# A decoder layer on one core: low parts of Wo on GpSimd in halves, TensorE's blocks of Wo five and three, pair 0's low part ahead of a scaling

## What is computed

```python
def _L0_attn_ref(x, w_qkv, w_o):
    ...
    qkv = x @ w_qkv
    ...
    xq = _apply_rope(xq)
    xk = _apply_rope(xk)
    keys = jnp.repeat(xk, N_REP, axis=1)
    values = jnp.repeat(xv, N_REP, axis=1)
    scores = jnp.einsum('bhsd,bhtd->bhst', xq, keys) * scale
    scores = jnp.where(causal, scores, -jnp.inf)
    probs = jax.nn.softmax(scores, axis=-1)
    out = jnp.einsum('bhst,bhtd->bhsd', probs, values)
    return out @ w_o

x = _layernorm(x + _L0_attn_ref(x, L0_attn_w_qkv, L0_attn_w_o), axis=-1)
```

## Time and profile before

| what | value |
|---|---|
| median of three runs | 1260.17 us (1259.99 to 1262.92) |
| profiled execution, its time | 1260.07 us |
| its span, first to last instruction | 1258.0 us |
| mean granted TensorE clock | 0.997 |
| TensorE busy | 1229.6 us (98%), 8134 matmuls |
| VectorE busy | 860.1 us (68%) |
| ScalarE busy | 580.6 us (46%) |
| GpSimd busy | 617.7 us (49%) |

### The profile page before, as it was taken

How to read it: one execution, slowest core, us unless ns; L and a number is a source line. 1 busy time by engine, 2 the same in 40 slices (tenths; PEclk the granted TensorE clock), 3 DMA queues, 4 the chain that set the end, 5 groups by cost and what they waited for, 6 DMA issues and landing times.

```text
span 1258.0 us, 25027 instructions
## 1 busy us (share of the span) xinstructions
PE 1229.6 (98%) x8134; PEld 1038.5 (83%) x8134; DVE 860.1 (68%) x2509; ACT 580.6 (46%) x1659; POOL 617.7 (49%) x522
## 2 busy tenths in 40 slices
PE   8999999999999999999999999999999999899997
PEld 6888889998788888888877887888888888678886
DVE  7999989565778888888776974253453635755654
ACT  5131213556777777777860222252342525532322
POOL 3512112458676776776750000454456554975552
PEclk9999999999999999999999999999999999999999
DMA  8154435364864344344443113317252444723221
GB/s 287 70 201 146 148 116 203 119 197 130 223 190 136 119 140 140 117 133 141 125 132 106 53 34 127 125 67 267 68 180 89 165 170 158 260 85 117 85 83 67
DMA packets 130833, 173.67 MB, mean 138 GB/s; under 512 B 36672, under 2 KB 91968, under 8 KB 130112
## 3 DMA queue, kind: packets, MB, share of 16 engines
q1 hardware_dynamic: 130752, 172.62, 42.2%
HBM read 115.94 MB, written 56.62 MB: 137 GB/s over the span
## 4 chain that ended last, share of the span: by engine, by line
PE 69%; POOL 14%; issue 10%; DMA 2%; DVE 2%; ACT 1%; SPq 1%; POOLq 0%; DVEq 0%; ACTq 0%
PE bank L773 14%; PE bank L775 13%; PE bank L774 13%; POOL prob L2165 10%; PE bank L859 5%; PE bank L1204 4%; PE bank L1206 4%; PE bank L1205 4%; PE bank L824 3%; PE bank L964 3%; POOL att_lo L2171 2%; PE bank L782 1%; PE bank L901 1%; PE bank L886 1%; PE bank L855 1%
## 5 line engine op out<-in xcount | busy, mean ns | idle before, releaser
L2165 POOL TENSOR_TENSOR prob<-prob,rinv 128x512 f32<-128x512 f32 x192 | 206.8, 1078 | 147.4 <-DVE rinv L1755 147.4
L1326 ACT ACTIVATE prob<-bank,nmax 128x256 f32<-128x256 f32 (+1 forms) x512 | 211.6, 429 | 76.0 <-DVE nmax L1747 70.0
L1747 DVE CUSTOM_DVE_ANT_0 bank<-bank,mask 128x256 f32<-128x256 f32 (+1 forms) x512 | 170.1, 385 | 38.0 <-PE bank L886 24.7
L901 PE MATMUL bank<-ident,prob 128*128 128x128 f32 x768 | 115.4, 273 | 1.3 <-ACT probT L1256 0.7
L901 PEld LDWEIGHTS bank<-ident,prob 128*128 128x128 f32 x768 | 94.5, 141 | 25.2 <-POOL prob L2165 2.4
L1326 ACT ACTIVATION_READ_ACCUMULATOR prob<-bank,nmax 128x1 f32 x512 | 109.7, 214 | 0.0
L964 PE MATMUL bank<-wo_hi,att_hi 128*128 128x512 f32 x256 | 104.3, 407 | 2.6 <-issue 2.6
L1902 DVE SCALAR_TENSOR_TENSOR k_lo<-bank,bA,k_hi 128x512 fp32r<-128x512 f32 x32 | 24.0, 751 | 120.9 <-ACT k_hi L1459 119.2
L886 PE MATMUL bank<-k,q 96*128 96x256 f32 (+1 forms) x512 | 104.2, 305 | 1.3 <-DMA vv<-v_scr 1.3
L964 PE MATMUL bank<-wo_hi,att_lo 128*128 128x512 f32 x256 | 101.3, 396 | 0.0
L964 PE MATMUL bank<-wo_lo,att_hi 128*128 128x512 f32 x256 | 101.2, 395 | 0.0
(11 more groups left out here) (221 smaller groups left out, 3247.0 us busy)
## 6 DMA issues: line engine op xcount, KB each, us to landing
q<-qk_scr SPq DMA_DIRECT2D x192, 128.0 KB, 2.4
x_st<-x_scr SPq DMA_DIRECT2D x32, 512.0 KB, 4.1
qk_scr<-rot SPq DMA_DIRECT2D x60, 256.0 KB, 2.6
xc_in<-x_cols SPq DMA_DIRECT2D x32, 256.0 KB, 4.7
y<-x SPq DMA_DIRECT2D x16, 512.0 KB, 3.6
x_scr<-y SPq DMA_DIRECT2D x16, 512.0 KB, 2.7
cx_in<-ctx_in SPq DMA_DIRECT2D x16, 512.0 KB, 4.9
x_scr<-x_st SPq DMA_DIRECT2D x16, 512.0 KB, 3.3
```

The costliest lines, as they stand in the source:

```text
L901: mm = nc.tensor.transpose(tb[:, at * P:(at + 1) * P], prob[:, k % 4, c:c + P], ident[:, :])
L1326: mm = nc.scalar.activation(prob[:, k % 4, i * keys:(i + 1) * keys], SBANK[pos][:, i * keys:(i + 1) * keys], ACT.Exp, bias=nmax[:, k % 4, ...
L1747: mm = nc.vector.tensor_tensor_reduce(part, part, mask[:, 2 * P - keys:2 * P], 1.0, BIGGEST, ALU.add, ALU.min, nmax[:, k % 4, i:i + 1])
L2165: nc.gpsimd.tensor_tensor(pr, pr, rinv[:, k % 4, 0:n].unsqueeze(2).to_broadcast([P, n, keys]), ALU.mult)\
```

## The change

Four things. The low parts of all eight blocks of Wo are taken by GpSimd, in halves of 512 columns with one semaphore (`wo_low`, `WO_LOW_STEPS`); block 5 goes from step 22 of batch 0 to step 3 of batch 1, blocks 6 and 7 come from VectorE to steps 5, 7 and 8 of batch 1. ScalarE makes the high parts of blocks 6 and 7 two steps earlier. TensorE takes five blocks for the first portion of `g` 0 and 1 and three for the second, and waits for both halves of a block. In every batch GpSimd takes the low part of outputs of pair 0 ahead of the scaling of step 23 instead of behind it.

```diff
-        LOW_STEP = {23: (0, 0), 0: (1, 1), 2: (1, 2), 6: (1, 3)}
-        WO_STEPS = {(0, 12): 2, (0, 14): 3, (0, 18): 0, (0, 19): 1, (0, 20): 4, (0, 21): 5, (1, 5): 6, (1, 7): 7}
-        WO_EARLY = sum(age == 0 for age, _ in WO_STEPS)
+        LOW_STEP = {0: (1, 1), 2: (1, 2), 6: (1, 3)}
+        WO_STEPS = {(0, 12): 2, (0, 14): 3, (0, 18): 0, (0, 19): 1, (0, 20): 4, (0, 21): 5, (1, 3): 6, (1, 5): 7}
+        WO_LOW_STEPS = {(0, 13): ((2, 0), (2, 1)), (0, 15): ((3, 0), (3, 1)), (0, 19): ((0, 0), (0, 1)), (0, 20): ((1, 0), (1, 1)),
+                        (0, 21): ((4, 0), (4, 1)), (1, 3): ((5, 0), (5, 1)), (1, 5): ((6, 0), (6, 1)), (1, 7): ((7, 0),),
+                        (1, 8): ((7, 1),)}
...
-            WO = [(g, kt, ps) for kts in (range(KT - 2), range(KT - 2, KT)) for g in (0, 1) for kt in kts for ps in range(3)]
+            WO = [(g, kt, ps) for kts in (range(KT - 3), range(KT - 3, KT)) for g in (0, 1) for kt in kts for ps in range(3)]
...
                     if g == 0 and ps == 0:
-                        if WO_TURN[kt] < WO_EARLY:
-                            pe.wait_ge(wo_lo_ready, WO_TURN[kt] + 1)
-                        else:
-                            pe.wait_ge(wo_lo2_ready, WO_TURN[kt] - WO_EARLY + 1)
+                        pe.wait_ge(wo_lo_ready, 2 * WO_TURN[kt] + 2)
...
-                    if age == 1 and (age, k - 1) in WO_STEPS:
-                        kt = WO_STEPS[age, k - 1]
-                        dve.wait_ge(wo_hi_ready, WO_TURN[kt] + 1)
-                        low(wo_lo[:, kt, :], wo_in[:, kt, :], wo_hi[:, kt, :]).then_inc(wo_lo2_ready, 1)
...
+            def wo_low(kt, half):
+
+                cols = slice(half * BANK, (half + 1) * BANK)
+                pool.wait_ge(wo_hi_ready, WO_TURN[kt] + 1)
+                nc.gpsimd.tensor_tensor(wo_lo[:, kt, cols], wo_in[:, kt, cols], wo_hi[:, kt, cols].bitcast(F32), ALU.subtract)\
+                    .then_inc(wo_lo_ready, 1)
...
+                    if k == SUB - 1:
+                        att_low(b, 0)
                     scale_probs(b, k)
...
-                    if age == 0 and (0, k - 1) in WO_STEPS:
-                        kt = WO_STEPS[0, k - 1]
-                        pool.wait_ge(wo_hi_ready, WO_TURN[kt] + 1)
-                        nc.gpsimd.tensor_tensor(wo_lo[:, kt, :], wo_in[:, kt, :], wo_hi[:, kt, :].bitcast(F32), ALU.subtract)\
-                            .then_inc(wo_lo_ready, 1)
                     if age == 1 and k == 4:
                         rope_low(item_pair(11))
+                    if age < 2 and (age, k) in WO_LOW_STEPS:
+                        for kt, half in WO_LOW_STEPS[age, k]:
+                            wo_low(kt, half)
```

More of the change, by code:

```diff
@@ L275, in decoder_layer @@
         t_step = sem("t_step")
-        wo_ld, wo_hi_ready, wo_lo_ready, wo_lo2_ready = (
-            sems("wo_ld", KT // 2), sem("wo_hi_ready"), sem("wo_lo_ready"), sem("wo_lo2_ready"))
+        wo_ld, wo_hi_ready, wo_lo_ready = (
+            sems("wo_ld", KT // 2), sem("wo_hi_ready"), sem("wo_lo_ready"))
         wq_first_ld, wq_ld, wq_hi_ready, wq_lo_ready = sem("wq_first_ld"), sem("wq_ld"), sem("wq_hi_ready"), sem("wq_lo_ready")
```

## The result

The changed kernel takes 1286.76 us (median of 4 runs, 1283.42 to 1289.29) where the kernel before takes 1261.08 (1259.99 to 1262.92): ratio 1.0188, 95% interval 1.0163 to 1.0212. It is slower by some 26 us, and far outside the range of the prediction. The profiled execution took 1286.05 us, span 1284.3. Lines of the changed kernel: transposes L903, scores L888, products of Wo L963 (L901, L886, L964 before); maxima L1746, reciprocals L1754 (L1747, L1755); scaling L2160, low part of `att` L2166, low part of Wo L2178 (L2165, L2171, L2191).

What follows compares the result with a forecast made beforehand. TensorE was taken as the limit in late batches, GpSimd in steps 3 to 8 of batch 1. The profiled 1260.07 less 1.0 gained at step 12 gave 1259.1, plus 0.1 for the median 1259.2; range 1256.7 to 1261.3.

Steps and rivals of the forecast that it cites:

- The stop of 2.56 us: TensorE's wait before the first product of Wo in batch 1, laid to GpSimd's order; the change would remove it.
- the new one of 1.7 us before the seventh product: Batch 1: TensorE would wait 1.7 us before block 2's first product, for the low part of pair 1 of `att`.
- Scores of step 6 at 316.0: Batch 1: with their load 2.3 us earlier, these scores start at 316.0 instead of 318.34, after a 0.8 us wait.
- The queue of loads: SP's stores of items 10 and 11, with loads queued behind, come 2.3 and 1.5 us earlier as GpSimd subtracts sooner.
- GpSimd as the bound of steps 3 to 8: Batch 1: GpSimd has 15.9 us of work against TensorE's 12.0, ending at 328.8; TensorE goes on at about 329.0.
- The sum for batch 1: After the stops, scores of step 12 start at 330.4 instead of 331.48, a gain of about 1.0 us.
- what is gained at 331.48 is kept to the end: After scores of step 12 in batch 1 TensorE is full, so the gain there lasts to the kernel's end.
- The second rival: The new stop at block 7 in batch 1 slows the clock; restart costs 1.6 us, total 1260.8; chance 0.17.
- Pair 0 ahead of step 23 in the other batches: GpSimd's new order in the later batches changes nothing either way, since TensorE had no wait there.
- VectorE loses two subtractions: Batch 1: taking them from VectorE leaves no pair excluding GpSimd; one scaling still stretched would cost 1.0 us.
- a new wait for scalings in the later batches: One of the signs named beforehand that would show the prediction wrong.

Runs made afterwards that it cites:

- version with two fillings: Changed kernel with two already-met waits put at the head of VectorE's program, so its loop begins where it did before; 1261.38 us, ratio 0.9992 to the kernel before.
- The run with early loads and high parts first: Changed kernel, Wo blocks 6 and 7 low parts back on VectorE, high-part products of blocks 2 to 4 first, loads ahead of stores; 1261.70 us, ratio 0.9992.
- the kernel before moved by two: Kernel before, without the change, four subtractions at VectorE's start joined into two so its loop begins two instructions earlier; 1297.34 us, ratio 1.0282.
- 250 fillings: Changed kernel with 250 already-met waits put at the head of VectorE's program; 1294.50 us, ratio 1.0257.

## Why the prediction was wrong

*The stop of 2.56 us, and the new one of 1.7 us before the seventh product: right* (none; 1.68). *Scores of step 6 at 316.0: right*, 316.82 less the common 0.6.

*The queue of loads: right.* SP's stores of items 10 and 11, which answer to the earlier trace rows, come 1.5 and 0.6 us earlier; with the common 0.6 these are 2.1 and 1.2, where 2.3 and 1.5 were worked out.

```profile
308.26 1.82 SPq L487 DMA_DIRECT2D qk_scr<-rot_last  x4
...
319.62 1.82 SPq L487 DMA_DIRECT2D qk_scr<-rot_last  x4
```

*GpSimd as the bound of steps 3 to 8: right.* Timeline of GpSimd in the changed kernel:

```profile
313.70 1.04 POOL L2160 TENSOR_TENSOR prob<-prob,rinv 128x512 f32<-128x512 f32 x1
314.70 2.52 POOL L2178 TENSOR_TENSOR wo_lo<-wo_in,wo_hi 128x512 fp32r<-128x512 f32 x2
317.17 1.04 POOL L2160 TENSOR_TENSOR prob<-prob,rinv 128x512 f32<-128x512 f32 x1
...
328.50 1.28 POOL L2178 TENSOR_TENSOR wo_lo<-wo_in,wo_hi 128x512 fp32r<-128x512 f32 x1
```

It starts at 313.70 (worked out: 312.9, and 0.6 for the common shift), a half costs 2.47 / 2 = 1.24 (taken: 1.22), and block 7's second half ends at 329.78 (worked out: 328.8). TensorE goes on at 329.83, not at 329.0.

*The sum for batch 1: its stops right, the gain smaller and not kept.* In the version with two fillings the clock does not fall behind the same stop, timeline of TensorE and windows of that run:

```profile
329.52 0.50 PE L963 MATMUL bank<-wo_hi,att_hi 128*128 128x512 f32 x1 [1.41 <-POOL wo_lo L2180]
...
330.91 0.48 PE L888 MATMUL bank<-k,q 96*128 96x256 f32 x2
...
362.08 0.49 PE L888 MATMUL bank<-k,q 96*128 96x256 f32 x2 [0.42 <-DMA vv<-v_scr]
```

```profile
331.00:335.00 4.00, 4.00 (x46) 3.28 (x44) 2.97 (x12) 3.10 (x10) 3.10 (x4) 1.00 0.79 201
```

The scores of step 12 start at 330.91, 0.57 us ahead of the kernel before (331.48), where 1.0 was worked out; 0.3 of what is missing is the later first product (306.21, not 305.9). Of the 0.57 only 0.12 are left at 362.08, the scores of step 3 of batch 2: they wait 0.42 us for their load, and in the kernel before they start at 362.20 without a wait. So "what is gained at 331.48 is kept to the end" fails in this trace: TensorE is not full there. The run with early loads and high parts first shows it with a larger gain, 2.30 us at step 12 (329.18) and 0.69 at the same scores of batch 2 (361.51). The median of the filled version is 1.1 us under the kernel before on the same chip, ratio 0.9992, near the 1.0 us forecast; but the interval takes in no gain at all, and with 0.12 us in the trace the agreement may be luck.

*The second rival: it happened in the profiled execution of the changed kernel and cost the 1.6 us named* (scores of step 11 start 0.30 us behind the filled version, at 327.75, and those of step 15 1.92 us behind, at 338.82), but not in the version with fillings, whose stop is as long (1.41 against 1.42). What tips the clock there stays open.

*Pair 0 ahead of step 23 in the other batches, "nothing either way": right as far as GpSimd's order goes.* The run with both fillings keeps this order and loses nothing.

***The step that failed is "VectorE loses two subtractions".*** It was costed as work: durations, what stood beside them, a port. Taking away instructions was held to be free or a gain. What was left out is that the instructions behind them move in the program. The loop of 283 instructions, which was kept over its turns with 958 or 959 ahead of it, is not with 957; VectorE stands 5.5 to 5.8 us at each of five turns, and each costs 4.8 us, 24 in all. No rival had this mechanism; the condition "a new wait for scalings in the later batches" would have shown it, and did (GpSimd's 4.33 at 412.87), but with VectorE behind it, not GpSimd's order. The profile before could have warned: its instruction queue moves no packet from 405 to 690, so the bodies of the loops stayed loaded, and a count of VectorE's instructions shows a body longer than one of the pieces measured above. On which side of an edge the loop lay, it does not show.

## What to carry to other kernels

An edit ahead of a loop moves the loop in its engine's program, and so can change its time by more than the edit itself: count the instructions ahead of the loop and in it, engine by engine, and read the instruction queue's packets per turn before and after. If a kernel gets slower by the same few microseconds at each turn of a loop, with an engine idle whose named releaser had long been done, put a few met waits ahead of the loop before you look for a cause in the order of the work. When a stop is taken away in a stretch where several engines are nearly late, look first what is late next.

## What the runs showed of the hardware

- VectorE's loop of 283 instructions is loaded again at each turn with 957, 1193 or 1207 instructions ahead of it (60 to 63 packets in the instruction queue over the span), and is kept with 958, 959, 1157 or 1179 (34 to 36 packets).
- A reload keeps VectorE standing 5.5 to 5.8 us between the last row of a pass and the first of the next with 957 ahead (changed kernel, five turns), 3.7 to 4.0 us with 1193 and 2.8 to 3.3 with 1207; where the loop is kept it is 0.34 (first turn). Of the 5.71 us at the first turn some 5.4 are not explained by the scores that it waits for. The five turns cost 4.8 us each in the changed kernel, 7.0 in the kernel before moved by two ((1297.34 - 1262.49) / 5; there GpSimd's order adds to it), and about 3.9 with 250 fillings (19.7 / 5).
- A met wait that stands alone costs VectorE some 68 ns (3.4 us for 50).
- Two stops of TensorE of 1.41 and 1.42 us at the same place were followed once by a clock of 1.00 and once by 0.50.
